# Another order of the row tiles in the first of four graph-attention layers

## The reference

```
Wh = x @ W
e  = leaky_relu((Wh @ a_src)[:, None] + (Wh @ a_dst)[None, :])
attention = softmax(where(adj > 0, e, very_negative), axis=1)
h  = attention @ Wh            # + bias in layer 1, elu in layers 0, 2, 3
x  = layernorm(x + h)
```

## Time and profile before

| what | us |
|---|---|
| median of 3 runs (lowest, highest) | 568.12 (564.32, 571.35) |
| the profiled execution, its own time | 572.38 |
| its span in the profile | 570.5 |
| busy: PE, ACT, DVE, POOL | 401.6, 395.5, 352.6, 280.7 |
| start of the last mask of the load (ACT) | 192.57 |
| first gather of layers 1, 2, 3 | 263.62, 361.49, 459.75 |

### The profile page before, as it was taken

One profiled execution on the slowest core, in us unless ns is written; L12 is line 12 of the kernel. 1 busy time (PEld: TensorE's weight loads), 2 busy tenths in 40 slices (PEclk: granted clock), 3 DMA queues, 4 the chain that ended last, 5 costly groups with the idle time before them and its releaser, 6 DMA issues.

```text
span 570.5 us, 10681 instructions
## 1 busy us (share of the span) xinstructions
PE 401.6 (70%) x3453; PEld 327.7 (57%) x3453; DVE 352.6 (62%) x1609; ACT 395.5 (69%) x868; POOL 280.7 (49%) x296
## 2 busy tenths in 40 slices
PE   2157364556997488874438999864999966499983
PEld 1145243346986378763227987643897754398662
DVE  2115579995689987885410488843068884206886
ACT  3288778869898736782355698737499963848883
POOL 0000001777634244003777776577777557777740
PEclk9998555555555558895867999968999986899997
DMA  7999999999999112001221222132222223212221
GB/s 295 385 428 427 424 429 424 405 395 329 352 354 363 50 15 40 19 19 34 26 28 27 29 48 46 37 46 28 29 28 48 42 47 38 30 27 39 45 39 33
DMA packets 20546, 84.86 MB, mean 149 GB/s; under 512 B 6083, under 2 KB 11462, under 8 KB 16262
## 3 DMA queue, kind: packets, MB, share of 16 engines
q1 hardware_dynamic: 10102, 73.15, 31.7%
q0 software_dynamic: 9344, 9.89, 12.9%
q10 hardware_dynamic: 1040, 1.08, 0.5%
HBM read 78.72 MB, written 5.37 MB: 147 GB/s over the span
## 4 chain that ended last, share of the span: by engine, by line
PE 22%; DVE 14%; ACT 13%; POOL 6%; issue 6%; DMA 2%; ACTq 0%; DVEq 0%
PE bank L714 10%; POOL xg L529 6%; PE bank L694 5%; ACT arena L872 5%; PE bank L675 3%; DVE x L1319 3%; ACT arena L858 3%; PE bank L673 2%; DVE stats L1301 2%; PE bank L710 1%; DVE arena L1238 1%; ACT arena L882 1%; DVE res L1298 1%; DVE mean_var L1304 1%; DMA xg<-table,index 1%
## 5 line engine op out<-in xcount | busy, mean ns | idle before, releaser
L529 POOL DMA_INDIRECT xg<-table,index x292 | 280.5, 961 | 269.6 <-DMA table<-wh 147.6
L846 ACT ACTIVATE arena<-arena,half 128x4096 bf16<-128x4096 int32 x31 | 114.9, 3706 | 29.5 <-DMA arena<-in_adj_t 29.5
L1238 DVE CUSTOM_DVE_ANT_0 arena<-bank,arena 128x256 f32<-128x256 f32 (+3 forms) x123 | 62.8, 522 | 104.5 <-ACT arena L858 103.7
L858 ACT ACTIVATE arena<-bank,sloped_own 128x256 f32<-128x256 f32 (+3 forms) x123 | 67.7, 555 | 58.2 <-PE bank L675 56.9
L694 PE MATMUL bank<-packed,arena 128*128 128x128 f32 x339 | 63.4, 307 | 18.7 <-ACT arena L882 16.6
L714 PE MATMUL bank<-xg,arena 128*128 128x64 f32 x486 | 70.0, 277 | 8.2 <-ACT arena L882 8.0
L714 PEld LDWEIGHTS bank<-xg,arena 128*128 128x128 f32 x486 | 61.2, 191 | 21.0 <-ACT arena L882 13.1
L675 PE MATMUL bank<-packed,xg 128*128 128x128 f32 x324 | 63.7, 299 | 0.0
L673 PE MATMUL bank<-off_row,wall 128*128 128x256 bf16 (+3 forms) x132 | 43.0, 326 | 24.5 <-DVE seg_max L1238 12.9
L694 PEld LDWEIGHTS bank<-packed,arena 128*128 128x128 f32 x339 | 43.0, 156 | 29.8 <-ACT arena L872 24.8
L882 ACT COPY arena<-bank 128x256 f32<-128x256 f32 (+3 forms) x123 | 53.8, 445 | 8.9 <-PE bank L694 6.0
(11 more groups left out here) (149 smaller groups left out, 759.7 us busy)
## 6 DMA issues: line engine op xcount, KB each, us to landing
arena<-in_adj_t SPq DMA_DIRECT2D x31, 2048.0 KB, 12.0
xg<-table,index POOLq DMA_INDIRECT x292, 2.9
table<-wh SPq DMA_DIRECT2D x24, 132.0 KB, 1.7
arena<-in_adj SPq DMA_DIRECT2D x1, 2048.0 KB, 12.9
table<-wh ACTq DMA_DIRECT2D x1, 1056.0 KB, 43.4
x<-in_x SPq DMA_DIRECT2D x1, 1024.0 KB, 15.0
out_x<-x SPq DMA_DIRECT2D x8, 128.0 KB, 1.9
packed<-in_c_packed SPq DMA_DIRECT2D x1, 312.0 KB
```

The costliest lines, as they stand in the source:

```text
L529: pool.indirect_dma_start(out=xg[:, c, :], out_offset=None, in_=table[l][0:rows, :], in_offset=bass.IndirectOffsetOnAxis(ap=index[:, c:c + ...
L846: nc.scalar.activation(masks[:, t % 2, :], arena[:, t % 3, :], ACT.Sign, bias=half[:, :]).then_inc(mask_made, 1)
L858: nc.scalar.activation(scores(l, n)[:, 0:m * P], score_ps[n % len(score_ps)][:, 0:m * P], ACT.Relu, bias=sloped_own[:, k:k + 1], scale=ALP ...
L1238: nc.vector.tensor_tensor_reduce(out=y, in0=score_ps[n % len(score_ps)][:, 0:m * P], in1=y, scale=-1.0, scalar=-FLOOR, op0=ALU.add, op1=AL ...
```

## The change

Layer 0 loads and computes the row tiles in another order; the batches are the same sets of tiles, listed otherwise, and `ORDER[0]` now follows `BATCHES` by itself.

```diff
-BATCHES = [(20, 4), (24, 4), (1, 3), (4, 4), (8, 4), (12, 4), (16, 4), (28, 2), (30, 2)]
+BATCHES = [(8, 4), (12, 4), (16, 4), (1, 3), (4, 4), (20, 4), (24, 4), (28, 2), (30, 2)]
...
-ORDER = [[DENSE] + list(range(20, 28)) + list(range(1, 20)) + list(range(28, TILES))] + [list(range(TILES))] * (LAYERS - 1)
+ORDER = [[DENSE] + TILE_AT] + [list(range(TILES))] * (LAYERS - 1)
```

## The result

| | us |
|---|---|
| kernel before, median of 4 runs (lowest, highest) | 568.69 (564.32, 571.35) |
| changed kernel, median of 4 runs (lowest, highest) | 552.15 (549.80, 552.77) |
| ratio, 95% interval | 0.9709 (0.9640 to 0.9778) |
| the same measured again, after 551.38, before 570.02 | 0.9666 (0.9623 to 0.9709) |
| profiled execution of the changed kernel, its span | 551.58, 549.7 |

The change is faster by 16.5 us, and by 18.6 when measured again. The forecast was 553.0. The two profiled executions lie 20.8 us apart, more than the medians, because the one before was 3.7 us above its median; places are therefore compared on the profiles, sizes on the ratios.

The account below looks back on a forecast made before the run. VectorE's list steps were taken to bound the load's end, late gathers the start of layer 1. Terms -10.4, -7.0 and +2.5 sum to -14.9 us, from the median 568.1 to 553 us; range 545 to 562.

Parts of the forecast that it names:

- Step 1: Start of layer 1: earlier group writes release the gathers sooner, so TensorE's wait for tile 1 closes; gain 10.4 us.
- The rival of the clock: Start of layer 1: TensorE's clock comes back too, the 24 transposes give 2.7 us more; 550.5 us, chance 0.09.
- Steps 2 to 4: The load of layer 0, late, early and middle parts together: a gain of 7.0 us, bounds 0 and 11.
- step 3: Early load: two heavier list batches add 13.0 us of VectorE work ahead of tile 0's maximum; loss taken as 1 us.
- step 4: Middle of the load, 123 to 167: four more chunks through TensorE, 2.8 us, of which 1.6 lost on the path.
- step 2: Late load, 167 to 208: lighter list steps take 9.6 us off VectorE, which is full there.
- the reserve that I left uncounted: Early load: the two-part batch of tiles 4 to 7 partly moves behind tile 0's maximum; no size given.
- It fits, barely: Early load, 45 to 123: VectorE's work with the added 13.0 us comes to 75.7 of 78 us.
- Step 5: Rounds behind the load: more chunks to transpose and multiply, 1.2 us, doubled for a possibly low clock; loss 2.5 us.
- The load gives nothing: Load: VectorE loses early what it gains late, or mask and DMA take over at once; 560 us, chance 0.13.
- half in time: Start of layer 1: gathers come only half in time, tile 1 still waits 5 us; 558 us, chance 0.07.
- VectorE as the bound of the front: Early load: VectorE's idle time is structural, so the 13.0 us stand in full; 571.6 us, chance 0.05.

Follow-up runs that it names:

- the second experiment: The changed kernel with room 16, not 8, for tiles 20 to 27, late in the load; 561.02 us, ratio 0.9826 to the kernel before.

## Why the prediction was right, step by step

The forecast of 553 held, and its largest step, the gathers, was shown alone. The sum was -14.9, and the profiles differ by 20.8: two of its losses were not there. That the median still came within 1 us of the forecast is luck in part. The profiled execution of before lay 3.7 us above its median, so that the 5.9 us that the sum lacks on the profiles are 1.6 on the medians (16.5), and 3.7 when measured again (18.6).

*Step 1, the start of layer 1: -10.4, measured 10.9 of span.* On the profiles the way from feature sum to products is 11.3 us shorter, of which 10.72 - 0.57 = 10.2 is the wait. Of the other 1.1, some 0.6 is the clock. Straight behind the gap the first score matmul took 0.61 us and the four behind it 1.06, at a granted clock of 0.50 (290.1 to 291.6); now they take 0.38 and 0.60, at 1.00 (270.1 to 271.0). ScalarE's first slope of tile 1 follows the start of that matmul by 1.50 us before and by 0.85 now. The Trainium skill ("TensorE: Matmul & The Clock Gate", Part 1) has an idle TensorE at half clock until activity releases it; the 0.61 and 0.38 agree. The 8 transposes behind are faster too (1.04 us now, 1.91 in the kernel with late gathers), but that gains nothing: ScalarE copies them only when it is through with its exponentials. The last 0.5 us lie in the 24 transposes, 4.97 us now and 5.50 before. In layer 2 of the changed kernel, where TensorE waits only 1.26 us for the gathers, they take 5.56; so it is not shown that closing the gap sped them up. I had said that no clock would come back, since I went by the 24 transposes only. The rival of the clock was right that some comes back, not where: it put 2.7 us on those transposes, and they gave at most 0.5.

*Steps 2 to 4, the load: -7.0, measured -9.7 at the last tile's search (207.72 to 198.01).* The masks of ACT show where. Before, then now, the first mask behind the exponential and the one at the end of the middle:

```profile
124.47 3.69 ACT L846 ACTIVATE arena<-arena,half 128x4096 bf16<-128x4096 int32 x1
...
167.59 3.71 ACT L846 ACTIVATE arena<-arena,half 128x4096 bf16<-128x4096 int32 x1
```

```profile
122.81 3.69 ACT L846 ACTIVATE arena<-arena,half 128x4096 bf16<-128x4096 int32 x1
...
167.99 3.71 ACT L846 ACTIVATE arena<-arena,half 128x4096 bf16<-128x4096 int32 x1 [0.46 <-PE bank L609]
```

The front ends 1.7 us earlier (step 3 said 1 later), the middle loses 2.1 (step 4 said 1.6), and from there to the last search 10.1 come back (step 2 said 9.6). Steps 2 and 4 were sized well, though no run shows step 4 alone; step 3 had the wrong sign, and the exponential came at 121.38, ahead of the 122 to 126 that the prediction named. VectorE's work up to 123 grew by 11.6 us (83.65 for 72.06), 10.2 of them from 45 on, where its idle time took them (5.1 of 78 us now, 15.3 before). What brings the exponential forward is the reserve that I left uncounted. Before, the two-part `mark_slots` of tiles 1 to 3 and of tiles 4 to 7 both stand ahead of the maximum; now only that of tiles 1 to 3 does, and a one-part one has come in for the other. One with two parts takes VectorE some 7 us (107.73 to 115.3 for tiles 4 to 7 before, 107.52 to 114.6 for tiles 1 to 3 now), one with one part some 3 (114.33 to 117.3 in the order with tiles 1 to 7 first). The kernel of before with heavy early lists keeps both two-part ones ahead, and its exponential is 4.8 us later than the changed kernel's (126.21 for 121.38); the order with tiles 1 to 7 first keeps both ahead too, and its exponential is 3.5 us later. No run moves this one step alone. "It fits, barely" was right, and right by the place of tiles 4 to 7.

*Step 5, the rounds behind the load: +2.5, measured -0.2.* From the last tile's search to round 50 it takes 265.98 - 207.72 = 58.3 us before and 256.12 - 198.01 = 58.1 now. By the prediction's own measure, from the last list step (221.65 before, 211.20 now), it takes 44.3 and 44.9 us, 0.6 more and not 2 to 3. Beside step 3 this is the term that was mis-sized most. The 1.2 us of more chunks are TensorE work in a stretch where TensorE is busy for 28.95 of 42 us now, 222 to 264, so idle time can have taken them; that is argued, not shown. The 1.2 us that I took for a colder clock on top had a price in the rows but no row for its coming; the granted clock in the 14 us from that search on is 0.62 now and 0.65 before, so next to nothing of it came.

*The rivals.* "The load gives nothing" falls with the second experiment, "half in time" with the 0.57 us; and VectorE as the bound of the front was far off in size: the order with tiles 1 to 7 first puts the most work there (85.9 us of VectorE up to 123, 83.7 in the changed kernel), and its exponential comes at 124.85, not 15 us late.

## What to carry to other kernels

Put the work that an engine can't hide where that engine has room, and ask of each place what is late next: here the heavier searches of two batches cost 9.5 us of span late in the load, and early in it, in the kernel of before, no more than the runs can tell. Follow a delay from mark to mark, not only from its start to its end: with tiles 1 to 7 first, 3.5 us in the front and 4.9 at layer 1 look like one delay, but in that profile most of the first was made up in the middle, and the second arose later. An order also decides when the data of the next stage are complete: the gathers' 10.9 us came from the moment at which the last of five writes was made, and nothing in the gathers themselves changed.

## What the runs showed of the hardware

The granted clock in the profile can be wrong for long stretches. In the second profile of the changed kernel it is 1.00 through the whole load, in that of before 0.50 from 123 on the earlier trace rows; yet the same products take the same time. Stretch 123 to 167 of the changed kernel's second profile, and in it the 64 products of tile 0 (line, shapes, count, busy us, mean ns), then the same in the profile before:

```profile
123.00:167.00 44.00, 39.77 (x382) 35.81 (x381) 29.22 (x113) 41.32 (x52) 32.22 (x33) 1.00 0.99 359
```

```profile
L714 PE MATMUL bank<-wh,slots 128*128 128x64 f32 x64 | 14.1, 414 | 0.0
```

```profile
L714 PE MATMUL bank<-wh,slots 128*128 128x64 f32 x64 | 14.1, 414 | 0.0
```

Where the clock was at the full level such products take 278 ns in the mean (68 of them from 222 to 246 in the changed kernel's first profile, granted clock 1.00). So TensorE ran at 1.2 GHz in that stretch of both, and the 1.00 is wrong; presumably the record lacks the event of a fall. The 1.00 from 45 to 123 in the first profile is no better: 32 score products of tile 0 take 419 ns in the mean there, and 420 in the profile before at 0.56, where at the full level they take 272 (264 to 272). First the changed kernel, then before:

```profile
L675 PE MATMUL bank<-packed,wh 128*128 128x128 f32 x32 | 8.5, 419 | 3.0 <-DVE seg_max L1238 2.4 <-issue 0.7
```

```profile
L675 PE MATMUL bank<-packed,wh 128*128 128x128 f32 x32 | 8.5, 420 | 0.0
```

The record can show 1.00 where it is wrong and go on showing it where it is right. In the kernel of before with heavy early lists it is 1.00 from 123 to 150, yet 8 transposes take 1.94 us at first and 1.11 soon after:

```profile
137.31 1.94 PE L694 MATMUL bank<-packed,score 128*128 128x128 f32 x8 [4.51 <-ACT slots L882]
...
143.64 1.11 PE L694 MATMUL bank<-packed,score 128*128 128x128 f32 x8 [0.38 <-ACT slots L882]
```

The Trainium skill ("TensorE: Matmul & The Clock Gate", Part 1) warns that the trace's events of the gate can't be fully trusted; this case agrees. The kernel with late gathers, at 0.54 from 45 to 123, reaches its feature sum 0.2 us ahead of the changed kernel at 1.00. A change of the clock between two profiles should be held against the durations of one kind of instruction before it is made a cause.
